# Gated block with expert routing on one Trainium2 core: h of eight units turned by DMA instead of TensorE, x1's rows loaded in pairs, two weight roundings moved to ScalarE

## The chip, the cores and the metric

The kernel runs on one core of a Trainium2 chip. The metric is the device time of one execution in microseconds (us); before the change it is 317.69 us, the median of three runs (317.64 to 318.01).

## What is computed

The reference, cut to what matters:

```python
x = x + tanh(g_xattn) * experts(layernorm(x), token_ids, ctx, ctx, ctx)   # 2048 rows of 512
x = x + tanh(g_ffn)   * ffn(layernorm(x))

def experts(h, ids, Wg, Wu, Wd):        # 4 experts, each weight 512 x 512; here Wg = Wu = Wd = ctx
    e = minimum(clip(ids, 0, 24999) // 6250, 3)
    y_e = (silu(h @ Wg[e].T) * (h @ Wu[e].T)) @ Wd[e].T      # each row takes the y of its own expert

def bit_linear(x, w, b):                # ffn = out(silu(gate(x)) * val(x)), hidden width 2048
    sx = 127 / clip(max|x| of the row, 1e-5);  gw = clip(mean|w|, 1e-5)
    return (clip(round(x * sx), -128, 127) / sx) @ (clip(round(w / gw), -1, 1) * gw).T + b
```

## The kernel before, in words

Every engine has its own program, written out by hand; an engine runs its instructions in that order and waits on semaphores.

**The unit stage (about 24 to 134 us).** The rows are sorted by expert into 19 units of 128 rows, numbered 0 to 18 in the code and in this text (so what the title of the change calls units 10 to 17 are units 9 to 16 here). The loop's step j, called slot j, does on TensorE (`slot`, L609): `turn_gu(j-1)`, four transposes of 128x128 f32; `product` a(j) (L574), twelve matmuls (a high part and a low part in f16 of the turned h against high and low parts of the weight, three passes of four); `turn_h(j+1)` (L558), four transposes of 128x128 f32 of the next unit's h; and `product` y(j-1), twelve matmuls. Around them, for the same slot:

- VectorE (loop after L1144): `gu_low(j-1)` (L1010), `x1_aggr(j-2)`, `gu(j)` (L1005), `h_low(j+1)` (L1001), `norm(j+2)` (L985, writes `h_sb`), `unit_stats(j+3)` (L991), `x1(j-1)` (L1014), `x1_bn_stats(j-1)`.
- ScalarE (`slot`, L804): `gu_hi(j-1)` (L777), `silu(j)` (L773), `h_hi(j+1)` (L769), and between them the work on the feed-forward weights as two tables lay it out: `sum_abs` (L781, sums of |w|, table SUMMED) and `sign_pair` (L792, the ternary weight, table SIGNED).
- GpSimd (loop at L458): the gather of unit j+4, the scatter of x1 of unit j-2 (two for units 8 to 10), `unit_rstd(j+3)`, a small copy, and `round_pair` (L430, table ROUNDED), which scales a pair of weight tiles and rounds it before `sign_pair`.
- SyncE issues, in this order: the twelve loads of 1 MB of the feed-forward weights (L257, the last four each when a gather has landed); the rows of x1, eight tiles of 257.5 KB (L267); the biases (L292 to L294); then the DMA transposes of the next stage (L273, 128x512 bf16; L283, 128x1024 bf16) and the last rows.

**The feed-forward stage (from 134 us)** works on tiles of 128 rows; the change does not touch its code. Its first gate product needs the first 16 sign pairs and the first turned tile of x.

Slots 1 to 14 are written out; slots 15 to 17 are a hardware loop on TensorE.

## Time and profile before

| | |
|---|---|
| median of three runs | 317.69 us |
| the profiled execution's own time | 316.65 us |
| its span, first to last instruction | 314.9 us (1.75 us lie outside it) |
| TensorE busy | 293.4 us, 93% |
| VectorE, ScalarE, GpSimd busy | 262.5, 214.4, 236.7 us |
| mean granted TensorE clock | 0.997 of full |

Times in the rows are microseconds from the span's start. PE is the matmul side of TensorE and PEld its weight loads, DVE is VectorE, ACT ScalarE, POOL GpSimd, SP SyncE; a q behind the name is the engine's sequencer, which issues DMAs. L585 is line 585 of the kernel before. DMA queue q1 is fed by SyncE, q0 by GpSimd's indirect transfers. A page's share of busy time is an average over stages, so the change is read from its own stretch, 67 to 134 us.

### The profile page before, as it was taken

The page shows a single profiled execution, that of the slowest core. Times are in us where ns is not written, and L with a number is a line of the kernel's source. Part 1 is how long each engine was busy: PE and PEld are TensorE (multiplying, and loading weights), DVE is VectorE, ACT ScalarE, POOL GpSimd, SP SyncE. Part 2 cuts the span into 40 slices and gives each one's busy share as a digit, 9 for nine tenths or more (in the row PEclk, how much of TensorE's full clock was granted, in tenths as well). Part 3 has the DMA queues.
Part 4 walks back from the last instruction along what each step waited for, and adds up shares of the span by engine and source line. Part 5 has one row for each costly group of instructions (what it writes and reads, how often), then busy time and mean ns, then how long its engine had stood idle before and what let it go on. Part 6 is the DMA issues. An engine that isn't in the chain of part 4 may idle for free.

```text
span 314.9 us, 5289 instructions
## 1 busy us (share of the span) xinstructions
PE 293.4 (93%) x1424; PEld 142.5 (45%) x1439; DVE 262.5 (83%) x499; ACT 214.4 (68%) x268; POOL 236.7 (75%) x260
## 2 busy tenths in 40 slices
PE   0979999999999999999889899999999999999981
PEld 0435555555555555544334344444444444444430
DVE  5869888868789986789998999998899889988850
ACT  4857688678866456786987788766976687664510
POOL 4554873798888779945776999898888987797722
PEclk9999999999999999999999999999999999999998
DMA  7689899674425822824152754546443542344171
GB/s 265 212 321 335 297 373 325 236 227 180 136 67 170 254 84 84 299 57 89 49 100 50 119 86 123 127 118 146 87 101 83 117 83 71 90 108 100 33 167 67
DMA packets 52549, 47.51 MB, mean 151 GB/s; under 512 B 44783, under 2 KB 44783, under 8 KB 50224
## 3 DMA queue, kind: packets, MB, share of 16 engines
q1 hardware_dynamic: 47968, 33.86, 39.6%
q0 software_dynamic: 4560, 13.40, 12.5%
q8 instruction: 10, 0.16, 0.2%
q14 instruction: 11, 0.09, 0.1%
HBM read 28.35 MB, written 10.00 MB: 122 GB/s over the span
## 4 chain that ended last, share of the span: by engine, by line
PE 82%; DVE 6%; DMA 5%; issue 2%; POOL 2%; ACT 1%; POOLq 0%; DVEq 0%
PE banks L585 31%; PE banks L652 16%; PE banks L661 16%; PE banks L676 14%; PE banks L592 3%; PE banks L562 2%; DMA raw<-in_ctx 2%; DVE raw L1117 1%; POOL w_both L443 1%; DMA out<-xg,raw 1%; DVE raw L1112 1%; DMA xg<-in_x,gather_at 1%; DVE xg L1142 1%; PE banks L548 1%; DMA tok<-in_itok_BxS 1%
## 5 line engine op out<-in xcount | busy, mean ns | idle before, releaser
L585 PE MATMUL banks<-w_both,turned 128*128 x444 | 102.0, 379 | 0.5 <-ACT turned L779 0.3
L443 POOL TENSOR_TENSOR w_both<-raw 128x1024 f32<-128x1024 f32 (+1 forms) x32 | 75.0, 2342 | 9.2 <-DVE raw L1112 7.2
L585 PEld LDWEIGHTS banks<-w_both,turned 128*128 128x128 f16 x444 | 43.4, 98 | 45.5 <-issue 1.6
L854 ACT ACTIVATE w_both<-w_both,magic,raw 128x1024 f32 (+1 forms) x31 | 38.2, 1234 | 36.4 <-DVE raw L1131 36.4
L676 PE MATMUL banks<-tern,xg 128*128 128x512 bf16 x248 | 59.6, 379 | 3.0 <-DVE xg L1142 1.0
L661 PE MATMUL banks<-tern,raw 128*128 128x512 bf16 x255 | 60.3, 379 | 1.3 <-DVE raw L1104 1.3
L652 PE MATMUL banks<-tern,raw 128*128 128x512 bf16 x251 | 59.9, 379 | 0.7 <-DVE raw L1112 0.4
L1104 DVE SCALAR_TENSOR_TENSOR raw<-banks,raw 128x1024 f32<-128x1024 f32 x32 | 40.9, 1278 | 5.7 <-issue 4.9
L1112 DVE SCALAR_TENSOR_TENSOR raw<-banks,raw 128x1024 f32<-128x1024 f32 x32 | 40.9, 1279 | 4.3 <-PE banks L661 4.3
L1117 DVE TENSOR_REDUCE raw<-w_both 128x1 f32<-128x1024 f32 x32 | 38.8, 1212 | 2.7 <-POOL w_both L443 2.6
L676 PEld LDWEIGHTS banks<-tern,xg 128*128 (+1 forms) x256 | 24.8, 98 | 33.7 <-DMA xg<-raw 1.8
L661 PEld LDWEIGHTS banks<-tern,raw 128*128 (+1 forms) x256 | 24.9, 98 | 32.0 <-DVE raw L1104 2.3
L652 PEld LDWEIGHTS banks<-tern,raw 128*128 (+1 forms) x256 | 25.0, 98 | 30.7 <-DVE raw L1112 0.9
L874 ACT ACTIVATE raw<-raw 128x1024 f32<-128x1024 f32 x32 | 33.4, 1045 | 7.0 <-DVE raw L1104 7.0
L490 POOL TENSOR_SCALAR w_both<-w_both,magic,one 128x1024 bf16<-128x1024 f32 x15 | 17.9, 1194 | 15.2 <-ACT w_both L854 15.2
L438 POOL TENSOR_SCALAR raw<-raw,inv_gam,magic 128x1024 f32<-128x1024 f32 x24 | 28.6, 1195 | 0.0
L794 ACT ACTIVATE tern<-raw,magic 128x1024 bf16<-128x1024 f32 x24 | 26.6, 1141 | 0.0
L1007 DVE SCALAR_TENSOR_TENSOR gu_sb<-banks,gu_sb 128x512 f32<-128x512 f32 x19 | 13.1, 687 | 13.8 <-ACT gu_sb L775 13.5
L346 POOL DMA_INDIRECT xg<-in_x,gather_at x19 | 20.3, 1066 | 5.1 <-issue 3.0
L775 ACT ACTIVATE gu_sb<-banks 128x512 f32<-128x512 f32 x19 | 11.3, 596 | 17.8 <-PE banks L585 17.8
L503 POOL DMA_INDIRECT out<-xg,raw x16 | 16.9, 1054 | 8.5 <-DVE xg L1142 6.2
L788 ACT ACTIVATE tern<-raw 128x1024 bf16<-128x1024 f32 x21 | 22.1, 1052 | 0.3
(121 smaller groups left out, 397.5 us busy)
## 6 DMA issues: line engine op xcount, KB each, us to landing
raw<-in_ctx SPq DMA_DIRECT2D x4, 1024.0 KB, 6.5
raw<-in_L_ffn_gate_w SPq DMA_DIRECT2D x4, 1024.0 KB, 7.4
raw<-in_L_ffn_val_w SPq DMA_DIRECT2D x4, 1024.0 KB
raw<-in_L_ffn_out_w SPq DMA_DIRECT2D x4, 1024.0 KB, 5.2
raw<-x_low SPq DMA_DIRECT2D x8, 257.5 KB, 4.4
raw<-x_high SPq DMA_DIRECT2D x8, 257.5 KB, 4.1
raw<-in_L_ffn_gate_b SPq DMA_DIRECT2D x1, 1024.0 KB, 5.4
raw<-in_L_ffn_val_b SPq DMA_DIRECT2D x1, 1024.0 KB, 8.1
```

The costliest lines, as they stand in the source:

```text
L438: nc.gpsimd.tensor_scalar(w, w, inv_gam[:, m:m + 1], magic[:, 0:1], ALU.mult, ALU.add).then_inc(rounded, 1)
L443: nc.gpsimd.tensor_tensor(z[:, t % 2, 2 * D * c:2 * D * c + width], g_sb[:, c, 0:width], v_sb[:, c, 0:width], ALU.mult).then_inc(z_made, 1)
L585: last = nc.tensor.matmul(acc[:, :], a[:, k * P:(k + 1) * P], flat(w[:, bass.ds(e4 + k, 1), :]), start=(k == 0 and i == 0), stop=(k == KD ...
L652: last = nc.tensor.matmul(ring[pair][:, b, :], flat(xiT[:, bass.ds(t % 2, 1), k, :]), tern[:, k * HC + 2 * c + b, :], start=(k == 0), stop ...
L661: last = nc.tensor.matmul(ring[pair][:, b, :], flat(xiT[:, bass.ds(t % 2, 1), k, :]), tern[:, G + k * HC + 2 * c + b, :], start=(k == 0), ...
L676: last = nc.tensor.matmul(to, flat(ziT[:, bass.ds(t % 2, 1), k, :]), tern[:, 2 * G + k, :], start=(k == order[0] * G // 2), stop=(k == (or ...
L794: nc.scalar.activation(flat(tern[:, bass.ds(2 * p, 2), :]), flat(raw[:, bass.ds(2 * p, 2), :]), ACT.Sign, bias=magic[:, 1:2]).then_inc(sig ...
L854: nc.scalar.activation(zq[:, a:b], flat(z[:, bass.ds(t % 2, 1), a:b]), ACT.Identity, scale=flat(sc[:, bass.ds(t, 1), 12:13]), bias=magic[: ...
L874: nc.scalar.activation(g_sb[:, c, :], g_sb[:, c, :], ACT.Silu).then_inc(s_made, 1)
L1104: v.scalar_tensor_tensor(g_sb[:, c, :], flat(ring[(4 * t + 2 * c + 1) % 3 if t else 0]), col(t, 3), bias_g[:, 2 * c * D:2 * (c + 1) * D], ...
L1112: v.scalar_tensor_tensor(v_sb[:, c, :], flat(ring[(4 * t + 2 * c + 2) % 3 if t else 1]), col(t, 4), bias_v[:, 2 * c * D:2 * (c + 1) * D], ...
L1117: v.tensor_reduce(col(t, 5 + c), z[:, t % 2, 2 * D * c:2 * D * (c + 1)], AX.X, ALU.max, apply_absolute_value=True).then_inc(zmax_made, 1)
```

## The change

- For units 9 to 16 (`H_DMA`), VectorE's `norm` writes h into the PSUM bank `hT_ps`; ScalarE's `h_hi` and VectorE's `h_low` make the f16 parts of the rows not yet turned, into `h16` (the bytes of `h_sb`), and SyncE turns both with one DMA transpose of 128x1024 f16 into one of two buffers. TensorE's four transposes for these units are gone, and `product` a(j) waits for the DMA. `norm(j+2)` and `unit_stats(j+3)` come ahead of `gu(j)` in slots 8 to 14, and h is prepared two units ahead.
- SyncE: the turns of units 9 to 14 stand behind the last weight load; then come the waits for the x1 rows, rows 0 and 1, the turn of unit 15, rows 2 and 3, the turn of unit 16, rows 4 to 7.
- ScalarE rounds pairs 8 and 9 itself, in slots 12 and 13, and sums all 24 pairs; VectorE's three `sum_abs` are gone. The tables SUMMED and SIGNED are laid out anew.
- TensorE's slots 15 to 17 are written out. `round_pair` on GpSimd waits load by load.

```diff
-    SUMMED = (0, 0, 2, 5, 8, 11, 13, 14, 15, 16, 18, 20, 21, 21, 21, 21, 21, 21, 21)
+    SUMMED = (0, 0, 2, 5, 8, 10, 13, 15, 16, 17, 18, 20, 22, 24, 24, 24, 24, 24, 24)
     ROUNDED = (0, 0, 0, 0, 0, 0, 2, 4, 6, 8, 8, 9, 10, 12, 14, 16, 20, 24, 24, 24, 24)
-    SIGNED = (0, 0, 0, 0, 0, 0, 0, 2, 4, 6, 8, 8, 9, 10, 12, 14, 16, 17, 18)
+    SIGNED = (0, 0, 0, 0, 0, 0, 0, 1, 3, 5, 7, 8, 9, 10, 12, 14, 16, 17, 18)
+    H_DMA = range(9, 17)
+    ACT_ROUNDS = range(8, 10)
...
+        h16 = h_sb[:, :].bitcast(f16)
+        hT_dma = tern[:, 2 * G + 6:2 * G + 10, :].bitcast(f16).rearrange("p (b i) d -> p b i d", b=2)
...
# SyncE, ahead of the twelve weight loads; called behind them
+            def turn_h(j):
+                sp.wait_ge(hTlo_made, j + 1)
+                if j >= H_DMA[0] + 2:
+                    sp.wait_ge(a_done, j - 1)
+                sp.dma_start_transpose(hT_dma[:, j % 2, :, :].rearrange("p i (k m) -> p (i k) m", m=P), h16).then_inc(h_turned, 16)
...
+            for j in H_DMA[:-2]:
+                turn_h(j)
             sp.wait_ge(signed, x_frees)
             stored_units(EARLY)
             sp.wait_ge(low_scattered, 16 * len(BOTH))
-            for t in range(EARLY):
+            load_rows(0)
+            load_rows(1)
+            turn_h(H_DMA[-2])
+            load_rows(2)
+            load_rows(3)
+            turn_h(H_DMA[-1])
+            for t in range(4, EARLY):
                 load_rows(t)
...
# TensorE, slot
+                    low_made = (hTlo_made, j + 1)
+                    if isinstance(j, int) and j in H_DMA:
+                        low_made = (h_turned, 16 * (j - H_DMA[0] + 1))
+                        pe.wait_ge(*low_made)
+                    else:
+                        pe.wait_ge(hThi_made, j + 1)
...
-                if after:
+                if after and not (isinstance(j, int) and j + 1 in H_DMA):
                     turn_h(j + 1)
...
-            with pe.Fori(GAMMA_SLOT[2] + 1, UNITS - 1) as j:
-                slot(j)
...
# ScalarE
             def h_hi(j):
+                if j in H_DMA:
+                    act.wait_ge(h_made, j + 1)
+                    if j == H_DMA[0]:
+                        act.wait_ge(hT_done, j)
+                    else:
+                        act.wait_ge(h_turned, 16 * (j - H_DMA[0]))
+                    nc.scalar.activation(h16[:, 0:D], hT_ps[:, :], ACT.Copy, scale=H_SCALE).then_inc(hThi_made, 1)
+                    return
...
+            def round_pair(p):
+                m = p // (G // 2)
+                act.wait_ge(gam_made, m + 1)
+                act.wait_ge(raw_loaded[p // 2], 16)
+                w = flat(raw[:, 2 * p:2 * p + 2, :])
+                nc.scalar.activation(w, w, ACT.Identity, scale=inv_gam[:, m:m + 1], bias=magic[:, 0:1]).then_inc(rounded_act, 1)
...
                 silu(j)
-                if 0 < j < UNITS - 1:
+                if 0 < j < UNITS - 1 and j + 1 not in H_DMA:
                     h_hi(j + 1)
+                if j + 2 in H_DMA:
+                    h_hi(j + 2)
...
# VectorE
+                if j in H_DMA:
+                    dve.wait_ge(hTlo_made, j)
+                elif j == H_DMA[-1] + 1:
+                    dve.wait_ge(h_turned, 16 * len(H_DMA))
+                v.tensor_scalar(hT_ps[:, :] if j in H_DMA else h_sb[:, :], unit_rows(j), mean_var[:, n, 0:1], rstd[:, n:n + 1],
...
+                early_norm = j + 1 in H_DMA and j + 2 in H_DMA
+                if early_norm:
+                    norm(j + 2)
+                    unit_stats(j + 3)
                 gu(j)
...
+                if early_norm:
+                    h_low(j + 2)
...
+                if j + 2 in H_DMA and not early_norm:
+                    h_low(j + 2)
...
-                if DVE_SUM <= j < DVE_SUM + PAIRS - ACT_SUMS:
-                    sum_abs(ACT_SUMS + j - DVE_SUM)
```

## Rows read from the trace of the kernel before

**Rows 1.** The page: engines' busy time, and the chain that ended last

```profile
PE 293.4 (93%) x1424; PEld 142.5 (45%) x1439; DVE 262.5 (83%) x499; ACT 214.4 (68%) x268; POOL 236.7 (75%) x260
PE 82%; DVE 6%; DMA 5%; issue 2%; POOL 2%; ACT 1%; POOLq 0%; DVEq 0%
```

**Rows 2.** The chain in order of time (start, us, what), slots 8, 10 and 15

```profile
67.05 0.44 PE banks L592 x4
67.49 2.59 PE banks L585 x12
70.08 0.44 PE banks L562 x4
...
73.10 0.44 PE banks L592 x4
...
79.16 0.44 PE banks L592 x4
...
82.30 0.49 PE banks L562 x4
...
112.80 0.44 PE banks L562 x4
```

**Rows 3.** SyncE's weight loads (ns min/median/max, first and last start us)

```profile
L257 SPq DMA_DIRECT2D raw<-in_L_ffn_out_w x4: 327/328/328, 49.7 to 69.0; - x4
```

**Rows 4.** DMA queues (packets, MB, share of 16 engines), 69 to 73 and 73 to 75 us

```profile
q1 hardware_dynamic: 119, 0.97, 73.9%
...
q0 software_dynamic: 158, 0.52, 66.6%
q1 hardware_dynamic: 25, 0.08, 10.1%
```

**Rows 5.** The 128x1024 DMA transposes: issue ns, landing; DMA busy tenths and q1, 299 to 301 us

```profile
L283 SPq DMA_TRANSPOSE xg<-w_both x30: 1231/1232/1247, 156.9 to 298.3; - x30
DMA to landing us min/median/max: 3.1/3.1/3.8
...
DMA  0000000002599999999999999999999999632000
...
q1 hardware_dynamic: 1056, 0.26, 68.2%
```

**Rows 6.** A transpose behind loads: issue, then packets of 128.5 to 130.5 and 130.5 to 132.5 us

```profile
128.58 6.77 SPq L273 DMA_TRANSPOSE raw<-raw  x2
...
DMA packets 162, 0.81 MB, mean 406 GB/s; under 512 B 26, under 2 KB 26, under 8 KB 88
...
DMA packets 749, 0.62 MB, mean 308 GB/s; under 512 B 580, under 2 KB 580, under 8 KB 748
```

**Rows 7.** Timeline of slot 9 (start, us, engine): ScalarE and VectorE

```profile
76.66 0.59 ACT L771 ACTIVATE turned<-banks 128x512 f16<-128x512 f32 x1
77.14 2.19 ACT L794 ACTIVATE tern<-raw,magic 128x1024 bf16<-128x1024 f32 x2
78.00 0.54 DVE L988 TENSOR_SCALAR h_sb<-xg,mean_var,rstd 128x512 f32<-128x512 f32 x1
79.27 0.74 DVE L1020 SCALAR_TENSOR_TENSOR x_sb<-banks,y_scale,xg 128x512 f32<-128x512 f32 x1
79.63 0.60 ACT L779 ACTIVATE turned<-banks 128x512 f16<-128x512 f32 x1 [0.31 <-issue]
80.12 1.05 ACT L788 ACTIVATE tern<-raw 128x1024 bf16<-128x1024 f32 x1
```

**Rows 8.** Groups by line (busy us, mean ns): the rounding on GpSimd, the nearest on ScalarE

```profile
L438 POOL TENSOR_SCALAR raw<-raw,inv_gam,magic 128x1024 f32<-128x1024 f32 x24 | 28.6, 1195 | 0.0
L854 ACT ACTIVATE w_both<-w_both,magic,raw 128x1024 f32 (+1 forms) x31 | 38.2, 1234 | 36.4 <-DVE raw L1131 36.4
```

**Rows 9.** Matmuls at the start: TensorE ns min/median/max

```profile
L554 PE MATMUL banks<-w_both x23: 379/634/634, 10.0 to 18.1; 128*128 128x512 f16 x23
```

**Rows 10.** Waits (us in total, times, longest): GpSimd for VectorE's unit statistics

```profile
POOL var_eps L382 <- DVE mean_var L999: 14.6, 11, 2.6
```

More of the change, by code:

```diff
@@ L175, in hT_of @@
         def hT_of(j):
+            if isinstance(j, int) and j in H_DMA:
+                return tuple(hT_dma[:, j % 2, i, :] for i in range(2))
             return hTs[isinstance(j, int) and j == 1]
@@ L432, in round_pair @@
                 m = p // (G // 2)
-                if p % (G // 2) == 0:
-                    pool.wait_ge(gam_made, m + 1)
-                    for q in range(4):
-                        pool.wait_ge(raw_loaded[4 * m + q], 16)
+                pool.wait_ge(gam_made, m + 1)
+                if p % 2 == 0:
+                    pool.wait_ge(raw_loaded[p // 2], 16)
                 w = flat(raw[:, 2 * p:2 * p + 2, :])
@@ L460, in _ @@
                 early_rounds = 1 if j < UNITS else 0
+                rounds = [p for p in rounds if p not in ACT_ROUNDS]
                 for p in rounds[:early_rounds]:
@@ L595, in sum_gamma @@
             def sum_gamma(m):
[L597 to L599 removed]
+                pe.wait_ge(abs_summed, G // 2 * (m + 1))
                 pe.wait_ge(consts32, 10)
@@ L638, in _ @@
             slot(0, before=False, after=False, between=turn_second)
-            for j in range(1, GAMMA_SLOT[2] + 1):
+            for j in range(1, UNITS - 1):
                 slot(j, gamma=GAMMA_SLOT.index(j) if j in GAMMA_SLOT else None)
-            with pe.Fori(GAMMA_SLOT[2] + 1, UNITS - 1) as j:
-                slot(j)
             slot(UNITS - 1, after=False)
@@ L1002, in h_low @@
                 dve.wait_ge(hThi_made, j + 1)
-                v.scalar_tensor_tensor(hT_of(j)[1], hT_ps[:, :], H_SCALE, hT_of(j)[0], ALU.mult, ALU.subtract).then_inc(hTlo_made, 1)
+                hi, lo = (h16[:, 0:D], h16[:, D:2 * D]) if j in H_DMA else hT_of(j)
+                v.scalar_tensor_tensor(lo, hT_ps[:, :], H_SCALE, hi, ALU.mult, ALU.subtract).then_inc(hTlo_made, 1)
             def gu(j):
@@ L1154, in _ @@
                     x_gamma(j - EARLY_SLOT - 2)
-                if 0 < j < UNITS - 1:
+                if 0 < j < UNITS - 1 and j + 1 not in H_DMA:
                     h_low(j + 1)
+                if early_norm:
+                    h_low(j + 2)
                 if j > EARLY_SLOT + 1:
@@ L1163, in _ @@
                     gamma(GAMMA_SLOT.index(j))
-                if j + 2 < UNITS:
+                if j + 2 < UNITS and not early_norm:
                     norm(j + 2)
@@ L1167, in _ @@
                     w_low(4)
-                if 2 <= j < UNITS - 3:
+                if 2 <= j < UNITS - 3 and not early_norm:
                     unit_stats(j + 3)
+                if j + 2 in H_DMA and not early_norm:
+                    h_low(j + 2)
                 if j == 5:
                     high_places()
-                if DVE_SUM <= j < DVE_SUM + PAIRS - ACT_SUMS:
-                    sum_abs(ACT_SUMS + j - DVE_SUM)
                 if j == UNITS - 1:
```

30 lines of the change are left out of this document (13 added, 17 removed).

## The prediction

> **What bounds the kernel now.** I read the page first: TensorE is busy 93% of the span and makes 82% of the chain that ended last [rows 1]. Then the same chain in order of time: from slot 2 to slot 18 it never leaves TensorE. A slot is 0.44 (`turn_gu`) + 2.59 + 0.44 (`turn_h`) + 2.59 = 6.06 us: slot 8 begins at 67.05, slot 9 at 73.10, slot 10 at 79.16 [rows 2]. So what TensorE drops there comes off the time, unless a new wait fills it. The other engines wait: ScalarE between its pieces, GpSimd for VectorE's unit statistics 11 times [rows 7, 10]. What must be read next is what a turn by DMA takes on SyncE's queue, and what stands ahead of it there.
>
> **The change part by part.**
>
> TensorE's transposes. Eight groups go, in slots 8 to 15, six at 0.44 us and two at 0.49, the first at 70.08, the last at 112.80 [rows 2], eight such rows: 8 x 0.45 = **-3.6 us**. A slot becomes 5.62 us.
>
> The DMA turn in a quiet slot. The nearest row is the same size in bf16: SyncE spends 1.23 us on the issue, it lands 3.1 to 3.8 us after it, and its data are moving for 1.36 us of all 16 engines (68.2% of 2 us), ending about 0.5 us ahead of the landing: the digits stop near 300.9, the landing of the issue at 298.3 is 301.4 [rows 5]. `h_low(j+2)` ends some 5.1 us into slot j: a(j) ends at 3.03, then silu 0.6, `h_hi` 0.5, `h_low` 0.7 and gaps. So the turn is issued at 5.2 and lands at 8.3 to 9.0, while a(j+2) begins at 2 x 5.62 + 0.44 = 11.7. The cover is 2.7 us or more. ScalarE's `h_hi(j+3)` asks for it earlier, 5.62 + 3.7 = 9.3 us: just enough. Cost 0.
>
> The first turn, unit 9. This one isn't quiet. In SyncE's program it stands behind the twelfth weight load, which starts at 69.0 [rows 3], for it waits for the gather of unit 11, which the change doesn't touch. So the turn is issued at about 69.4, right behind 1 MB. That load keeps q1's engines busy until after 73: 119 packets in 69 to 73, the last 25 in 73 to 75, while gather and scatter on q0 take 66.6% of 73 to 75, or 1.33 us of all engines [rows 4]. Does a transpose wait for loads ahead of it on its queue? One row can tell: turn_x(0), issued at 128.58 behind the bias loads, has hardly any small packets in the first 2 us (26) and 580 in the next 2, when the loads are done [rows 6]; a quiet one moves its packets 1.1 to 2.6 us after the issue [rows 5]. So it waits. From 73.0 on there remain 0.2 (load) + 1.33 (q0) + 1.36 (turn) = 2.9 us, to 75.9, and 0.5 to the landing: 76.4 if the turn is last of all. If q0 took nothing from it: 73.4 + 1.36 + 0.5 = 75.3. I take **76.0**, nearer to the end where both share, since q0 is served all through 73 to 75.
> TensorE wants it at 73.10 - 0.44 + 0.44 = 73.1: it stands for **2.9 us** (2.2 to 3.3).
>
> What queues up behind that wait. ScalarE's `h_hi(10)` waits for the same turn, because both use `h16`; behind it stand two sign pairs (2.19 us) and `gu_hi(8)` (0.6) [rows 7]. Counted from the landing L: `h_hi` starts at L+0.05, the signs at L+0.53, `gu_hi(8)` at L+2.65, ready at L+3.2; TensorE is through a(9) at L+2.65, so it stands **0.6 us** more for y(8). Then VectorE: `gu_low(8)` at L+3.25, `norm(11)`, `unit_stats(12)` and `gu(9)`, each of 0.5 to 0.9 us, end at L+6.05, where y(8) ended at L+5.85: **0.2 us** more. Slot 10 so begins at L+6.05 = 82.05, against 79.16 before [rows 2]: 2.9 us late. From there the lag is gone: ScalarE has 5.1 us of work (1.8 + one sum 1.1 + two signs 2.2) in slots 9 and 10 each.
> With the 6 groups of slots 10 to 15 (2.7 us) the stage ends 2.9 - 2.7 = **0.2 us later** than before. In other terms: 3.8 us of stands (with roundings) against 3.6 saved.
>
> ScalarE in slots 12 and 13. Its own three pieces 1.8 us, two sums (1.05 and the read of the sum, 1.14 with it) 2.3, a sign pair 1.1, and the new rounding, whose nearest rows are 1.23 (ScalarE, same tile) and 1.20 (GpSimd) [rows 7, 8]: 6.4 us in a slot of 5.62, twice. Lag 1.6 us; `gu_hi` may come 1.9 us late (turned at 0.44, needed at 3.03, 0.6 long). With waits between the pieces `gu_hi(13)` ends about where it is needed: **+0.2 us**, between 0 and 1.6. Slot 14 has 4.0 us and takes it back. VectorE loses three sums and gets `norm` writing PSUM, an operation the trace lacks; PSUM-touching ones of this size take up to 0.74 against 0.54 [rows 7], so at most 0.2 a unit, with some 0.3 free ahead of `gu`. GpSimd loses 2 x 1.2 us [rows 8]; it waits for VectorE anyway [rows 10], cost 0. If its two-round passes should bind, the cover is the whole slot by which `rstd` runs ahead.
>
> Rows of x1 and turns 15 and 16. Two tiles of 257.5 KB ahead of a turn are half the load that delays unit 9, and are issued some 3 us before the turn is ready; the turn has 2.7 us of cover more. Cost 0, up to 0.5. Rows 4 to 7 land near 117, about when GpSimd wants them. Writing out slots 15 to 17: 0. The feed-forward stage hangs on TensorE's last unit slot and moves with it.
>
> Sum, against the profiled 316.65: -3.6 + 3.8 + 0.2 = +0.4, so 317.0; the median of the runs lies 1.04 above the profiled execution: 318.05, told as **318.0**.
>
> A rule that speaks against this change: the Trainium skill, page "VectorE: DVE Perf Modes", section on rules for kernel authors, says to use TensorE for a 128x128 transpose where PSUM will do as its target, and its section on the three transpose paths gives 1309 ns for one by DMA. Eight such blocks one after another would be 10.5 us a unit, and the slots would be bound by it: an estimate from that page, 8 x (10.5 - 6.06) = +36 us. The trace disagrees: eight blocks land in 3.1 us [rows 5].
>
> **The rivals.**
>
> A. The turn lands in time everywhere, unit 9 too. For: nothing in the code orders the data of two transfers. Against: [rows 6], and q1's engines are full up to 73 anyway [rows 4]. Then -3.6 + 0.2: **314.3**. Chance 0.10.
>
> B. The wait is there, but at its short end and without followers: L = 75.3, the signs don't hold `gu_hi(8)`. -3.6 + 2.2 + 0.1 = -1.3: **316.4**. For: bounds above. Against: the order of ScalarE's program. Chance 0.08.
>
> C. Slower: ScalarE, late from unit 9's turn, doesn't recover before slots 12 and 13, and their overload falls on TensorE in full. It decides once ScalarE enters slot 12 more than 0.3 us late, for then all 1.6 us show, through `gu_hi`, and some 0.4 more by `silu` and `gu`. 318.0 - 0.2 + 2.0: **319.8**. For: 5.1 and 5.2 of 5.62 us in slots 10 and 11 leave little to recover with. Against: slot 9's slack. Chance 0.12.
>
> D. Slower: TensorE's clock falls in the stand at unit 9. The first matmuls of the run, after idle time, took 634 ns at median against 379 later [rows 9], the lower of the two levels (1.2 and 2.4 GHz); no idle stretch of 3 us occurs later. Some 12 to 16 matmuls at 0.21 us more: +3.0, **321.0**. Chance 0.04. The Trainium skill, page "TensorE: Matmul & The Clock Gate", Part 1, has the clock fall after idle time; by that rule D is what a stand at the long end would give, and no row here shows it.
>
> **How the numbers follow.** The forecast's case has 0.66; its own range is 317.3 to 318.8 (L from 75.3 to 76.4, ScalarE's 0 to 0.6). The range that should hold 8 in 10 leaves out A, D and the far edges: 316.2 to 319.6. A measurement of this kernel can tell some 0.2%, 0.64 us, from no change: same is 317.05 to 318.33. Faster: A, B and 0.04 of the forecast's case, 0.22. Slower: C, D and 0.22 of it, 0.38. Same: the other 0.40.
>
> **What would show it.** In the profile after: no L562 rows in slots 8 to 15 and slots of 5.62 us (right), TensorE idle some 3 us before a(9), released by the DMA or by ScalarE's chain, ScalarE idle as long before `h_hi(10)`; the small packets of the first turn after 73.4; slot 10 beginning near 82. The prediction is wrong if the first turn's packets move by 71 to 72.5 (A), if stands appear at slots 13 and 14 (C), or if matmuls after the stand take over 600 ns (D).

## The result and the profile after

The changed kernel takes **322.48 us** (median of 4 runs, 321.74 to 325.57) against 317.85 of the kernel before on the same chip (317.64 to 318.94): ratio 1.0147, 95% interval 1.0095 to 1.0198. It is slower by 4.6 us, where no change was forecast. Its profiled execution took 322.68 us with a span of 320.9, against 316.65 and 314.9 of before: 6.0 us to explain.

The page of the changed kernel, busy time and the chain that ended last [rows 1]:

```profile
PE 295.2 (92%) x1406; PEld 139.5 (43%) x1406; DVE 261.9 (82%) x496; ACT 219.4 (68%) x276; POOL 234.2 (73%) x258
...
PEclk9999999997999999999999999999999999999978
...
PE 71%; DMA 10%; DVE 9%; issue 3%; ACT 2%; POOL 2%; POOLq 0%; DVEq 0%; SPq 0%; ACTq 0%
```

TensorE has fewer instructions and is busy 1.8 us longer (the trace of before lacks 14 of its matmul records, so the difference isn't exact). The PEclk line says why: two dips, one in the slice near 76 us and one in the last two; the very last slice dips in before too, behind its last matmul. DMA has gone from 5% of the chain to 10%.

The chain in order of time, slots 9 and 10 [rows 2]:

```profile
69.82 0.33 SPq L269
...
70.19 6.39 DMA tern<-h_sb
...
76.71 7.04 PE banks L606 x24
83.75 0.44 PE banks L613 x4
```

The turn of unit 9, issued right behind the twelfth weight load, lands 6.39 us later, and the chain runs through it. The timeline of the same stretch (start, us, engine, line; in brackets the idle time and what ended it) [rows 7]:

```profile
73.34 0.66 PE L613 MATMUL banks<-ident,gu_sb 128*128 128x128 f32 x4
...
76.67 0.60 ACT L798 ACTIVATE h_sb<-banks 128x512 f16<-128x512 f32 x1 [4.75 <-DMA tern<-h_sb]
76.71 4.45 PE L606 MATMUL banks<-w_both,tern 128*128 x12 [2.72 <-DMA tern<-h_sb]
...
80.55 0.78 DVE L1037 TENSOR_SCALAR banks<-xg,mean_var,rstd 128x512 f32<-128x512 f32 x1
81.00 2.75 PE L606 MATMUL banks<-w_both,turned 128*128 x12
```

TensorE stands 2.72 us, and then the twelve matmuls of a(9) take 4.45 us, where twelve take 2.75 in the next row. Windows of 3 us (busy time of PE, PEld, DVE, ACT, POOL, then the granted clock, DMA share, GB/s) show it:

```profile
73.00:76.00 3.00, 0.94 (x6) 0.42 (x4) 0.28 (x1) 0.00 (x0) 2.89 (x5) 1.00 1.09 318
76.00:79.00 3.00, 2.29 (x6) 0.91 (x7) 1.67 (x3) 2.33 (x3) 1.48 (x3) 0.65 0.39 133
79.00:82.00 3.00, 3.00 (x12) 1.23 (x11) 2.48 (x6) 2.66 (x6) 1.49 (x2) 0.78 0.77 175
```

The eight turns, by their line (duration of the issue; landing min/median/max) [rows 5]:

```profile
L258 SPq DMA_TRANSPOSE tern<-h_sb x8: 1232/1236/1331, 70.2 to 113.5; - x8
...
DMA to landing us min/median/max: 3.1/3.4/6.4
```

The slowest is the first. The next slowest are those issued at 83.3 and 100.1, with 4.7 and 5.3 us to the landing; more of them below.

The other half is at the end of the program, which the change doesn't touch. The last two DMA transposes and the last 16 matmuls, first of before, then of the changed kernel:

```profile
300.88 2.61 SPq L283 DMA_TRANSPOSE xg<-raw  x2
301.38 1.90 PE L676 MATMUL banks<-tern,xg 128*128 128x512 bf16 x8 [0.64 <-DMA xg<-w_both]
304.17 3.75 PE L676 MATMUL banks<-tern,xg 128*128 128x512 bf16 x16 [0.90 <-DMA xg<-raw]
```

```profile
304.07 3.37 SPq L295 DMA_TRANSPOSE xg<-raw  x2
304.57 1.90 PE L698 MATMUL banks<-tern,xg 128*128 128x512 bf16 x8 [0.64 <-DMA xg<-w_both]
308.60 5.31 PE L698 MATMUL banks<-tern,xg 128*128 128x512 bf16 x16 [2.13 <-DMA xg<-raw]
```

From the issue of the pair to the last 16 matmuls it takes 3.29 us before and 4.53 after, and the 16 take 5.31 instead of 3.75. What else is on the queues there, 305 to 306.5 us of the changed kernel:

```profile
q1 hardware_dynamic: 944, 0.24, 84.6%
q8 instruction: 1, 0.02, 3.9%
```

One packet of q8 lies among those of the transposes. The page has 11 such packets with 0.18 MB in the whole run, 16 KB each, and calls their kind "instruction". They come 13 to 31 us apart, but for 84 us (191 to 275) in which TensorE goes round its loop of the feed-forward stage. I read them as the fetch of TensorE's next instructions; experiments 5 and 10, which add instructions to TensorE and nothing else, move them. In before the last was at 282 us. In the changed kernel it is at 306. Two more lie beside the two slow turns named above, at 85.3 and 103.4.

**Where 6.0 us went.** I took the start of each slot from the timelines (`turn_gu`'s first matmul) and subtracted. Slot lengths in us, and the part from the last `turn_gu` to the end of the span:

| slot | 8 | 9 | 10 | 11 | 12 | 13 | 14 | 15 | 16 to 18 | end part |
|---|---|---|---|---|---|---|---|---|---|---|
| before | 6.05 | 6.05 | 6.23 | 6.05 | 6.06 | 6.05 | 6.23 | 6.05 | 17.86 | 181.4 |
| after | 6.15 | 10.25 | 5.75 | 5.62 | 5.61 | 5.62 | 6.73 | 5.93 | 17.86 | 184.2 |

Slots 8 to 18 are 2.9 us longer (+4.20 in slot 9; -1.8 in slots 10 to 13; +0.5 in slots 8, 14 and 15 together), the end part 2.8, and 0.3 lies ahead of slot 8.

### The profile page after: what moved, and what is told of

It is laid out like the page before. It is cut to its first block, busy times and chain, and to the rows that moved or that the text cites. A ratio compares the mean times of both kernels' runs of the same rounds, so it can differ in the third digit from the quotient of the medians.

```text
span 320.9 us, 5259 instructions
## 1 busy us (share of the span) xinstructions
PE 295.2 (92%) x1406; PEld 139.5 (43%) x1406; DVE 261.9 (82%) x496; ACT 219.4 (68%) x276; POOL 234.2 (73%) x258
## 4 chain that ended last, share of the span: by engine, by line
PE 71%; DMA 10%; DVE 9%; issue 3%; ACT 2%; POOL 2%; POOLq 0%; DVEq 0%; SPq 0%; ACTq 0%
PE banks L606 22%; PE banks L674 16%; PE banks L683 16%; PE banks L698 14%; DMA tern<-h_sb 4%; DMA xg<-in_x,gather_at 3%; DMA raw<-in_ctx 2%; PE banks L613 2%; DMA out<-xg,raw 1%; DVE raw L1162 1%; POOL w_both L463 1%; DVE raw L1157 1%; PE banks L583 1%; DVE xg L1187 1%; PE banks L569 1%
## 5 line engine op out<-in xcount | busy, mean ns | idle before, releaser
L606 PE MATMUL banks<-w_both,turned 128*128 x348 | 80.0, 379 | 1.1 <-ACT turned L809 0.8
L698 PE MATMUL banks<-tern,xg 128*128 128x512 bf16 x256 | 61.5, 387 | 3.8 <-DMA xg<-raw 2.1
L606 PEld LDWEIGHTS banks<-w_both,turned 128*128 128x128 f16 x348 | 34.0, 98 | 38.3 <-issue 3.3
L606 PE MATMUL banks<-w_both,tern 128*128 x108 | 26.6, 398 | 3.3 <-DMA tern<-h_sb 2.7
L458 POOL TENSOR_SCALAR raw<-raw,inv_gam,magic 128x1024 f32<-128x1024 f32 x22 | 26.2, 1192 | 0.0
L820 ACT ACTIVATE tern<-raw 128x1024 bf16<-128x1024 f32 x24 | 25.3, 1053 | 0.3
```

What stands on the lines that cost most here:

```text
L458: nc.gpsimd.tensor_scalar(w, w, inv_gam[:, m:m + 1], magic[:, 0:1], ALU.mult, ALU.add).then_inc(rounded, 1)
L606: last = nc.tensor.matmul(acc[:, :], a[:, k * P:(k + 1) * P], flat(w[:, bass.ds(e4 + k, 1), :]), start=(k == 0 and i == 0), stop=(k == KD ...
L698: last = nc.tensor.matmul(to, flat(ziT[:, bass.ds(t % 2, 1), k, :]), tern[:, 2 * G + k, :], start=(k == order[0] * G // 2), stop=(k == (or ...
```

## The experiments

Sixteen kernels were run, in four groups, each group on one chip with runs of the kernel before beside it (its medians 318.01, 318.32, 317.54 and 317.70). Single runs of one kernel scatter by some 2 us either way (before: 315.97 to 320.34), so a reading rests on the profile's slot lengths, with the ratio beside it. Part of that scatter lies ahead of the change: in the profiled executions of experiments 5, 6, 8, 9, 10 and 12 slot 3 is 6.65 to 7.80 us long instead of 6.05, and in that of 4 slot 4 is 7.40. In 9 TensorE stands 1.46 us there for VectorE's x1, and VectorE stood 2.73 us for a gather that landed late. The change isn't needed for it (kernels 4 and 10 are the kernel before at that place), nor are the short matmuls of some kernels (4 and 6 have none). But five of the six long slots 3 stand in kernels with short matmuls at the start, so a tie to these isn't ruled out. "End part" is always the time from the last `turn_gu` to the end of the span.

### 1. The turn of unit 9 ahead of the weight load

```diff
             for n in range(12):
+                if n == 11:
+                    turn_h(H_DMA[0])
...
-            for j in H_DMA[:-2]:
+            for j in H_DMA[1:-2]:
                 turn_h(j)
```

> Only edit to the changed kernel: unit 9's turn is issued ahead of the twelfth weight load instead of behind it. Theory Q (the turn's data wait behind 1 MB on the same queue): it lands 3.1 to 3.8 us after its issue at about 68.7, so by 72.5; TensorE's stand of 2.7 us ahead of a(9) and ScalarE's of 4.75 are gone, and with the stand the 12 matmuls at half clock (4.45 us for 2.6). Slot 18 then begins near 126 instead of 131.1 (127.9 before). For the end there are two theories. F: the late transpose landing at the end (4.5 us against 3.3 before) comes from a TensorE instruction fetch that falls on it, and it stays, as TensorE's program is the same length: about 317.5. N: the end was chance: 315.0. Rival to Q (a first DMA transpose is slow by itself): the stand stays and the time is about 322.

Measured: 317.61 us, ratio 0.9973 (0.9939 to 1.0007). Slot 9 takes 5.94 us instead of 10.25:

```profile
71.30 2.76 PE L608 MATMUL banks<-w_both,turned 128*128 x12 [0.15 <-ACT turned L811]
74.11 0.66 PE L615 MATMUL banks<-ident,gu_sb 128*128 128x128 f32 x4
74.68 1.30 SPq L258 DMA_TRANSPOSE tern<-h_sb  x1
74.86 2.76 PE L608 MATMUL banks<-w_both,tern 128*128 x12
```

No stand, and the clock stays up. So the place on SyncE's queue costs the stand, and this one edit takes back the whole loss of the unit stage: its slots 8 to 18 sum to 65.3 us, 4.2 less than in the changed kernel and 1.3 less than before's 66.6. The first row shows a small thing: slot 8 has no `turn_h(9)`, yet it keeps 6.16 us, because y(7) now waits for ScalarE. The end part is still 182.5, with a q8 packet at 303 us and 2.09 us of stand; here the last 16 matmuls took 3.63 us, so the clock stayed up.

### 2. Turns by DMA from unit 10 on

```diff
-    H_DMA = range(9, 17)
+    H_DMA = range(10, 17)
```

> Only edit: the turned units are 10 to 16, seven instead of eight; unit 9 is turned on TensorE as before. Theory Q: the turn of unit 10 is issued when the weight load is done, no stand, seven times 0.45 us saved: slot 18 begins 0.5 us later than with unit 9's turn moved ahead, about 126.5. By F the end still costs some 2.8 us (318.0), by N not (315.5). Rival to Q (a first transpose is slow by itself): a stand of some 2.7 us now stands ahead of a(10), about 322.

Measured: 319.84 us, ratio 1.0048 (1.0016 to 1.008), profiled 318.05. No stand at unit 10: its turn is issued at 74.4, and a(10) begins at 79.88. Slot 9 takes 6.16 us. Slots 10 to 12 stayed at 6.16, 6.27 and 6.01, so this kernel has less of the saving than the count of its turns says (its last `turn_gu` is at 133.7, and the expectation for the unit stage missed by 1.5 us). TensorE waits there in short gaps, the longest 0.26 us for ScalarE's `gu_hi`; the rest isn't explained. The end part is 182.6: its q8 packet is at 303 us, and TensorE stands 2.20 us. The first slot without `turn_h` doesn't get shorter, neither here (slot 9) nor in experiment 1 (slot 8).

### 3. TensorE kept busy in the stand

```diff
                         low_made = (h_turned, 16 * (j - H_DMA[0] + 1))
+                        if j == H_DMA[0]:
+                            keep_warm(12)
                         pe.wait_ge(*low_made)
```

> Only edit: 12 matmuls of 128x512 on a free bank, ahead of the wait for unit 9's turn, so that TensorE works while it would stand. Theory C (TensorE's clock fell because of the stand): a(9)'s matmuls take 379 ns again, 2.6 us instead of 4.45, and slot 10 begins near 82.0 instead of 83.75; the end as in the changed kernel or moved by the 24 instructions more; 320.7. Rival (the slow matmuls of a(9) have another cause, as their operands just landed by DMA): they stay at over 600 ns and the time is 322.5.

Measured, in the profiled execution (319.36 us): slot 9 takes 8.83 us instead of 10.25.

```profile
74.39 2.76 PE L575 MATMUL banks<-w_both 128*128 128x512 f16 x12
76.99 2.75 PE L606 MATMUL banks<-w_both,tern 128*128 x12
```

```profile
76.00:79.00 3.00, 3.00 (x16) 1.35 (x15) 1.86 (x3) 2.52 (x3) 2.06 (x3) 1.00 0.29 111
```

Same landing of the turn (6.42 us), granted clock 1.00, a(9) in 2.75 us instead of 4.45. The clock's share of slot 9 is 1.4 (the slots) to 1.7 us (the matmuls). Its median, 322.98 of 4 runs (319.36 to 327.32; ratio 1.018, 1.0099 to 1.0262), says nothing of a gain: the stand itself varies between executions. The profiled ones with the turn behind the load have 2.72 us (changed kernel), 2.38 (experiment 5), 1.63 (11) and 6.75 (14).

### 4 and 5. The unrolling alone, and instructions added

The kernel before with slots 15 to 17 written out as the change has them:

```diff
-            for j in range(1, GAMMA_SLOT[2] + 1):
+            for j in range(1, UNITS - 1):
                 slot(j, gamma=GAMMA_SLOT.index(j) if j in GAMMA_SLOT else None)
-            with pe.Fori(GAMMA_SLOT[2] + 1, UNITS - 1) as j:
-                slot(j)
```

> The kernel before with one part of the change alone: TensorE's slots 15 to 17 written out. Theory F: some 170 instructions more ahead of the end, so its last fetch, at 282 before, comes at about 264 and one more at about 292, ahead of the last transposes by 8 us: no change of the time, 0 to 0.3 us. Rival (written-out slots cost more than a loop): each of slots 15 to 17 longer than 6.06 us, 318.5 or more.

Measured: 317.51 us, ratio 0.9964 (0.9938 to 0.999). Slots as before, but for slot 4; the last q8 packets moved to 268 and 293 us, clear of the last transposes; end part 181.3. The unrolling alone costs nothing, and by itself it does not bring a fetch to 306 us either. That takes the other part of the change with it: the turns of eight units, 64 instructions fewer ahead of the end.

The changed kernel with 48 short matmuls (96 instructions with their weight loads) at TensorE's start:

```diff
             pe.wait_ge(consts16, 3)
+            for _ in range(48):
+                nc.tensor.matmul(a_ps[:, 0:4], ones16[:, :], ones16[:, 0:4], start=True, stop=True)
```

> Only edit: 48 tiny matmuls in TensorE's idle time at the start, 96 instructions more in its program. Nothing moves in the unit stage. Theory F (an instruction fetch of TensorE that falls on the last DMA transposes makes them land late): the last fetch, at 305.5 in the changed kernel, moves some 10 us ahead, to 293 to 297; the last transposes land 3.3 us after the issue, the clock stays up: 319.7 to 320. Theory N (chance, or something else of the change): the end stays slow, 322.5.

Measured: 321.77 us, ratio 1.0095 (1.0067 to 1.0123), profiled 322.96. The last q8 packet is at 295; the last 16 matmuls begin 3.29 us after the issue of the pair and take 3.84 us, as in before. But the time is not won: packets now lie on the turns issued at 78.5 and 95.0, which land 4.5 and 5.2 us after their issue instead of 3.1 and 3.7, and slot 13 takes 6.93; one more at 136 us falls on the first x transposes of the feed-forward stage, and TensorE stands 1.46 us there (end part 183.1). The expectation of 319.7 to 320 missed. Adding instructions at the start moves every fetch at once. The stand at unit 9 was 2.38 us in this execution, and the granted clock did not fall behind it: a(9) took 2.76 us and slot 9 took 9.09.

### 6 and 7. The two roundings

The kernel of experiment 1 with both roundings back on GpSimd:

```diff
-    ACT_ROUNDS = range(8, 10)
...
-                rounds = [p for p in rounds if p not in ACT_ROUNDS]
...
+                act.wait_ge(rounded, p + 1)
```

> Edit on the kernel with unit 9's turn ahead of the last weight load: GpSimd again rounds pairs 8 and 9. Theory S (two sums, a rounding and a sign are too much for ScalarE in slots 12 and 13, and it shows in slot 14, 6.57 us long where 5.82 would do): slot 14 comes back to 5.9, the unit stage ends 0.7 us earlier; about 317.0. Rival FU (slot 14 is long because an instruction fetch at 99.3 falls on unit 14's turn, and h_hi(15) waits for it): slot 14 stays above 6.3 us, 317.6.

Measured: 317.62 us, ratio 0.998 (0.995 to 1.0011). Slot 14 falls from 6.57 to 5.75 us, so ScalarE's work has a part in it. Slots 16 and 17 rise to 6.31 and 6.77 for a reason that I hadn't thought of:

```profile
121.69 0.78 ACT L903 ACTIVATE banks<-raw 128x512 f32<-128x512 f32 x1 [2.40 <-POOL raw L438]
122.41 2.17 ACT L833 ACTIVATE tern<-raw,magic 128x1024 bf16<-128x1024 f32 x2
124.49 0.57 ACT L809 ACTIVATE turned<-banks 128x512 f16<-128x512 f32 x1
```

GpSimd's step for the first tile (L438) has slid behind the roundings, ScalarE waits 2.40 us for it, and `gu_hi` and two signs are queued behind that wait. This is a cost of the roundings on GpSimd with shorter slots. The sum is a draw. Its turn of unit 14 has a fetch beside it as in experiment 1, so the rival that this fetch alone makes slot 14 long is out.

The roundings alone on ScalarE, in the kernel before:

```diff
+    ACT_ROUNDS = range(8, 10)
...
+                rounds = [p for p in rounds if p not in ACT_ROUNDS]
```

> The kernel before with one part of the change alone: ScalarE rounds pairs 8 and 9, in slots 12 and 13, the rest as before. Theory S: in the slots of 6.06 us with at most one sum beside it ScalarE has 5.3 us of work, so nothing shows: within 0.3 us of the kernel before, slots 12 to 14 at 6.06, 6.05 and 6.23. Rival (the rounding on ScalarE costs by itself, 1.24 us each): slots 13 and 14 longer by 0.5 or more, 318.7.

Measured: 318.75 us, ratio 1.001 (0.998 to 1.0041); slots 6.05 to 6.23 as before. In slots of 6.06 us ScalarE has room for them; in slots of 5.62 it hasn't.

### 8, 9 and 12. Early turn with more instructions at the start

Experiment 1 with 15 (8) and 57 (9) short matmuls at the start, and (12) with 57 and eight more matmuls ahead of the wait for the last transposes.

> Edit on the kernel with unit 9's turn ahead of the last weight load: 15 tiny matmuls in TensorE's idle time at the start, 30 instructions more, so that its fetches come some 3.3 us sooner. Theory F: the last fetch falls at about 299, ahead of the last two transposes (issued at 300.6 and 302), which land 3.3 us after the issue again; the end, from TensorE's last unit transposes to the last instruction, is 181.4 to 181.7 us instead of 182.5, and those of the unit stage fall between turns: 316.3. Rival N: the end stays at 182.5, 317.6.

> The kernel after with the turn of unit 9 issued ahead of the twelfth weight load, and 57 short matmuls (114 instructions) at TensorE's start, so that its program is fetched at other moments: by the spacing of the earlier traces at about 73, 91 and 288 us instead of 81, 99 and 302. Theory F (a fetch of TensorE's instructions during a DMA transpose lengthens it): no turn of h and not the last pair of transposes has a fetch beside it; the last pair lands within 3.4 us of its issue, the part behind the last turn of gu takes 181.3 us instead of 182.5, the turns land after 3.1 to 3.7 us; median about 1 us below the kernel before, 316 to 317. Rival (the end is late for another reason, such as the order in which the feed-forward stage finds its weights): the part behind the last turn of gu stays at 182.4 to 183.4 us, and the median stays at 317.5.

> The kernel with the early turn of unit 9 and the 57 short matmuls at the start, and eight matmuls of 512 columns ahead of TensorE's wait for the last two transposes (1.7 us). If the transposes are in time (0.9 us of stand) the eight matmuls cost 0.8 us and the time lies that much above the kernel without them; if they are late, they cost nothing and keep the clock up. Both theories: unit stage as in the kernel without them, 1.5 to 2 us shorter than before; median 316 to 317.5.

Measured: 317.48 us (ratio 0.9972, 0.9933 to 1.0012), 318.21 (1.0018, 0.9993 to 1.0043) and 318.43 (1.0035, 1.0007 to 1.0064). All three expectations on the total missed. In each a fetch fell at another place; slot 3 was long in the profiled executions of all three as well (7.10 to 7.80 us), and that costs as much again. The edit at TensorE's start (57 in place of 15 in 9 and 12), and that of 12 at its end:

```diff
+            for _ in range(15):
+                nc.tensor.matmul(a_ps[:, 0:4], ones16[:, :], ones16[:, 0:4], start=True, stop=True)
...
+            for _ in range(8):
+                nc.tensor.matmul(o_of(t), tern[:, 2 * G, 0:P], tern[:, 2 * G + 1, :], start=True, stop=True)
             down(t, 1, to=o_of(t), order=(1, 0))
```

In 8 the q8 packet came at 300.7 us and fell on the transposes of 298.7, one pair earlier: 2.13 us of stand, the clock fell, end part 183.4. In 9 and 12 the last transposes were in time as expected (0.91 us of stand in 9), but a packet at 131 us fell on the first x transposes. Of experiment 9:

```profile
128.41 9.23 SPq L287 DMA_TRANSPOSE raw<-raw  x2
133.35 0.60 PE L617 MATMUL banks<-ident,gu_sb 128*128 128x128 f32 x4
135.51 1.90 PE L678 MATMUL banks<-tern,raw 128*128 128x512 bf16 x8 [1.55 <-DMA raw<-raw]
```

That is 1.55 us of stand where before has none, and the end part is 183.1. The slots, 5.62 to 5.97 from 9 to 15, were as good as foreseen.

These two also tell the causes of the long slot 14 apart. In 9 and 12 ScalarE has both roundings, and no fetch lies behind the issue of unit 14's turn, which lands after 3.7 us: slot 14 takes 5.97. In experiment 6 it has neither, with the turn late: 5.75. In experiment 1 it has both, with the turn late: 6.57. So either alone costs 0.2 us or less, and the two together 0.8.

### 10 and 15. A fetch put onto the last transposes of the kernel before

The kernel before, nothing of the change in it, with 43 (10) and 60 (15) short matmuls at the start:

```diff
+            for _ in range(43):
+                nc.tensor.matmul(a_ps[:, 0:4], ones16[:, :], ones16[:, 0:4], start=True, stop=True)
```

> The kernel before, nothing of the change in it, with 43 short matmuls (86 instructions) at TensorE's start. The last fetch of its program was at 282 us and the one behind it would have been past the end, 31 us later; 86 instructions more bring that one to about 302.5, onto the last two transposes (issued 300.9). Theory F: these land 4.4 to 4.6 us after their issue instead of 3.3, TensorE stands about 2.1 us instead of 0.9 ahead of the last 16 matmuls, the part behind the last turn of gu takes 182.5 us (clock stays up) to 184.2 us (it falls) instead of 181.4; the slots of the unit stage stay 6.05 to 6.23. Rival: 3.3 us and 181.3 us as before, so that the long end comes from the change's own work.

> The kernel before with 60 short matmuls (120 instructions) at TensorE's start, 34 instructions more than in the kernel whose last fetch was at 275 us: the one behind it comes at about 302 us, onto the last two transposes (issued about 301 to 302.7). Theory F: they land 4.4 to 4.6 us after issue, TensorE stands about 2.1 us instead of 0.9, and the part behind the last turn of gu takes 182.5 us (the clock stays up) to 184.2 us (it falls) instead of 181.4, with nothing of the change in the kernel. Rival: 181.4 us. If the fetch misses them again: 181.4 us by both, and no answer.

Measured: in 10 the last packet is at 275 us and none follows; end part 181.3, ratio 1.0016 (0.9989 to 1.0043). It missed its aim and tells only that the short matmuls cost nothing that the times show; slot 3 took 7.31 us in its profiled execution. In 15 packets came at 271 and 301 us:

```profile
301.77 2.61 SPq L283 DMA_TRANSPOSE xg<-raw  x2
303.76 7.01 PE L678 MATMUL banks<-tern,xg 128*128 128x512 bf16 x24 [2.13 <-DMA xg<-w_both]
```

and in 300.5 to 302.5 us:

```profile
q1 hardware_dynamic: 962, 0.24, 63.0%
q8 instruction: 1, 0.02, 2.8%
```

TensorE stands 2.13 us, the end part is 183.3 instead of 181.4, the slots are 6.05 to 6.23 as in before, and the median is 319.02 beside 317.70 (ratio 1.0023, 0.9993 to 1.0052, so the times alone show no difference; the profile does). It hit the pair ahead of the last one and not the last, but it shows the point: a long end comes without any of the change's work, by where the fetch falls.

How much of it is the clock, the profile of experiment 3 tells. There a fetch fell on the same pair, and TensorE stood 2.09 us:

```profile
305.29 5.35 PE L700 MATMUL banks<-tern,xg 128*128 128x512 bf16 x24 [2.09 <-DMA xg<-w_both]
```

The clock stayed up, the 24 matmuls took 5.35 us instead of 7.01, and the end part is 181.7. So at this pair the late landing itself costs 0.3 us and the clock 1.7.

### 11. TensorE kept busy ahead of the last transposes

```diff
             t = TILES - 1
+            for _ in range(10):
+                nc.tensor.matmul(o_of(t), tern[:, 2 * G, 0:P], tern[:, 2 * G + 1, :], start=True, stop=True)
             down(t, 1, to=o_of(t), order=(1, 0))
```

> The kernel after with ten matmuls of 512 columns on a free bank ahead of TensorE's wait for the last two transposes (2.2 us at the upper clock). If the granted clock falls because TensorE stands there: the last 16 matmuls take 3.7 us instead of 5.3 and the profiled execution ends 1.2 to 1.6 us earlier, 321.2, with the transposes still landing 4.4 us after their issue and the stand at unit 9 as before (slot 9 at 10.2 us). If it falls for another reason, the last 16 stay at 5 us. Against this: if the transposes are in time the ten matmuls themselves cost up to 1 us.

Measured: 320.8 us, ratio 1.0098 (1.0062 to 1.0134), profiled 320.88.

```profile
303.99 3.42 SPq L295 DMA_TRANSPOSE xg<-raw  x2
304.49 1.90 PE L698 MATMUL banks<-tern,xg 128*128 128x512 bf16 x8 [0.64 <-DMA xg<-w_both]
306.23 2.32 PE L747 MATMUL banks<-tern 128*128 128x512 bf16 x10
308.53 3.63 PE L698 MATMUL banks<-tern,xg 128*128 128x512 bf16 x16
```

The transposes are still late (308.53 is 4.54 us after the issue), but the last 16 take 3.63 us instead of 5.31 and the end part is 182.5 instead of 184.2. So the 2.8 us of the end are 1.2 for the late landing and 1.6 for the clock. Slot 9 took 8.34 us in this execution and not the expected 10.2: the stand was 1.63 us, and no fall of the clock followed.

### 13 and 14. The fetch moved inside the feed-forward stage

54 short matmuls at three places where TensorE stood 0.41, 0.42 and 0.88 us for VectorE, so that the unit stage keeps its program. 13 has the early turn as well, 14 only this:

```diff
+            def short(count):
+                for _ in range(count):
+                    nc.tensor.matmul(o_ps[:, 0:4], ones16[:, :], ones16[:, 0:4], start=True, stop=True)
...
-            ffn_slot(2, 0, downs=False)
-            ffn_slot(3, 1, start_down=True)
+            ffn_slot(2, 0, downs=False, shorts=(13, 13))
+            ffn_slot(3, 1, start_down=True, shorts=(28, 0))
```

> The kernel after with the turn of unit 9 issued ahead of the twelfth weight load, and 54 short matmuls (13, 13 and 28) in the feed-forward stage, at three places where TensorE stood 0.41, 0.42 and 0.88 us for VectorE, on a bank that nothing uses there. The unit stage keeps its program and so its fetches; the later fetches come some 10 us sooner (about 262 and 290 us, not 271 and 302). Theory F (a fetch during a DMA transpose lengthens it): the last two transposes land 3.3 us after their issue, TensorE stands 0.9 us there instead of 2.1, the part behind the last turn of gu takes 181.2 to 181.6 us instead of 182.5, slots 13 and 14 stay at 5.8 and 6.6; profiled time near 316.3, median 0.5 to 1.2 us below the kernel before. Rival (the end is late for another reason): 182.5 us.

> The kernel after, with only the same 54 short matmuls in the feed-forward stage. Theory F: the fetch of 305 us comes at about 293; the last two transposes land 3.3 us after issue, the last 16 matmuls take 3.7 us, the part behind the last turn of gu takes 181.2 to 181.6 us instead of 184.2; the stand at unit 9 stays (slot 9 at 8.3 to 10.3 us), so the profiled time is 318.6 to 320.2. Rival: 183 to 184 us behind the last turn of gu, and 322.

Measured, 13: **316.19 us**, ratio 0.9951 (0.9925 to 0.9977), profiled 315.46. The last packets are at 261 and 286 us, and

```profile
299.80 2.61 SPq L297 DMA_TRANSPOSE xg<-raw  x2
300.30 1.90 PE L700 MATMUL banks<-tern,xg 128*128 128x512 bf16 x8 [0.64 <-DMA xg<-w_both]
303.07 3.66 PE L700 MATMUL banks<-tern,xg 128*128 128x512 bf16 x16 [0.88 <-DMA xg<-raw]
```

with an end part of 181.4. Slot 14 is still 6.63 us.

14: 319.44 us, ratio 1.0044 (1.0014 to 1.0075), against 1.0147 of the changed kernel; end part 181.2. The end is mended with nothing else touched, and what is left is the unit stage. Its runs lie between 317.57 and 324.61. The profiled one, 324.19, is one of the two longest, and shows what made it so:

```profile
80.44 5.27 PE L606 MATMUL banks<-w_both,tern 128*128 x12 [6.75 <-DMA tern<-h_sb]
```

In this execution the turn of unit 9 landed 9.7 us after its issue, not 6.4, and TensorE stood 6.75 us; slot 9 took 15.1, and the expectation (8.3 to 10.3) missed. The load isn't the whole reason: its last packet ends at 75.8 us, against 75.1 in the changed kernel. But of the turn's packets 179 come after 76.5, up to 79.9, beside those of GpSimd's transfers, where in the changed kernel none comes after 76.0:

```profile
q0 software_dynamic: 120, 0.40, 70.5%
q1 hardware_dynamic: 179, 0.04, 7.2%
```

(76.5 to 80 us.) Why they came so late isn't shown, nor how often it happens: the other runs have no trace.

### 16. One of the two roundings back on GpSimd

Experiment 13 with

```diff
-    ACT_ROUNDS = range(8, 10)
+    ACT_ROUNDS = range(8, 9)
```

> The kernel with the early turn of unit 9 and the 54 short matmuls in the feed-forward stage, and of the two roundings only the first (pair 8) on ScalarE, the second back on GpSimd. With both on ScalarE slots 13 and 14 took 5.8 and 6.6 us; with both on GpSimd slots 16 and 17 took 6.3 and 6.8, because ScalarE stood 2.4 us for a step of GpSimd that had slid behind the roundings. Theory: each rounding on ScalarE costs the slots 13 and 14 about half of 0.9 us, so slot 14 is near 6.1 us and slots 16 and 17 near 6.1 and 6.3: no gain or up to 0.5 us. Rival (the long slot 14 is the late turn of 96.8 us alone, with a fetch beside it): slot 14 stays at 6.5 us or more.

Measured: **314.58 us** (6 runs, 314.25 to 315.37), ratio 0.9892 (0.986 to 0.9923): 3.1 us faster than the kernel before and 1.6 faster than experiment 13. Slots 13 to 15 take 5.76, 6.08 and 5.62 us (5.65, 6.63 and 5.94 in 13), 16 and 17 stay at 6.05. The timeline of ScalarE in slots 13 and 14:

```profile
101.61 0.60 ACT L806 ACTIVATE h_sb<-banks 128x512 f16<-128x512 f32 x1 [1.08 <-DMA tern<-h_sb]
102.11 1.05 ACT L828 ACTIVATE tern<-raw 128x1024 bf16<-128x1024 f32 x1
103.06 0.19 ACT L828 ACTIVATION_READ_ACCUMULATOR tern<-raw 128x1 f32 x1
103.15 1.14 ACT L845 ACTIVATE tern<-raw,magic 128x1024 bf16<-128x1024 f32 x1
104.19 0.58 ACT L817 ACTIVATE turned<-banks 128x512 f16<-128x512 f32 x1
```

The turn is just as late as in 13 (a packet of q8 lies beside it; it lands 5.6 us after its issue, 5.2 in 13), yet without the rounding of 1.23 us between sum and sign `gu_hi` ends 3.16 us after the start of `h_hi` (104.77) and not 4.43 (105.56). So slot 14 was ScalarE's overload behind a late turn, both of them, and the rival that it was the late turn alone falls. The profiled executions differ by 0.77 us (314.69 against 315.46), which the slots account for (0.75); the medians differ by more, and that rest isn't explained.

## Why the prediction was wrong, step by step

The forecast was 318.0, between 316.2 and 319.6. It came to 322.48. Against the forecast's sum (317.0 for the profiled execution, 322.68 measured) 5.7 us are missing:

| step | forecast, us | measured | missed |
|---|---|---|---|
| quiet turns, slots 10 to 13 | -1.8 | -1.8 | 0 |
| slot 8 | -0.45 | +0.1 | 0.55 |
| stand at unit 9 and followers, less the group of slot 9 | +3.3 | +4.2 | 0.9 |
| slots 14 and 15, and ScalarE's overload | -0.7 | +0.4 | 1.1 |
| feed-forward stage "moves with it" | 0 | +2.8 | 2.8 |
| ahead of slot 8 | 0 | +0.3 | 0.3 |

- **Quiet turns: right.** Five of the eight land in 3.1 to 3.7 us, and slots 11 to 13 take the forecast 5.62 us; the one issued at 83.3, which lands after 4.7, has cover enough. On the rule about transposes by DMA that the prediction names, the trace of the changed kernel says the same as [rows 5]: a quiet turn of eight blocks lands in 3.1 us.
- **The queue behind the weight load: right.** [rows 6] told it. Landing 6.39 us after the issue, 6.6 forecast; stand 2.72 us, 2.9 forecast. Rival A falls with the packets: from 72 to 74.4 us q1 moves 94 of 8 KB and none under 512 B, and 1072 of these come by 76. Experiment 1 shows that the order on the queue is the cause. That the stand came so near is in part luck, as it was 1.63 to 6.75 us in the other executions with this order. The followers were over-sized: with the clock up (experiment 3) slot 9 took 8.83 us where the forecast's steps give 9.4.
- **The clock, rival D, came at a chance of 0.04.** This is the first failed step. The stand was forecast at nearly 3 us, [rows 9] showed matmuls at the lower level behind idle time, and "no idle stretch of 3 us occurs later" in the kernel before was a reason to take the risk seriously, not to set it low. It was over-sized too: 1.4 to 1.7 us and not 3.0, because the twelve matmuls of a(9) took 0.14 us more each (4.45 instead of 2.75 us together) and not 0.21, the clock coming back meanwhile (granted 0.65 from 76 to 79 us, 0.78 from 79 to 82). The Trainium skill, "TensorE: Matmul & The Clock Gate", Part 1, has the clock fall after idle time. The trace agrees at 2.72 us of stand. Of the four profiled stands at this place (1.63, 2.38, 2.72 and 6.75 us, in experiments 11 and 5, the changed kernel and experiment 14) the two longer ones brought a fall and the two shorter ones did not. So the chance was nearer to one half than to 0.04.
- **Slot 8: a saving that a queue took.** I subtracted 0.45 us from every slot. In the first one ScalarE's `h_hi(9)` stands 1.79 us for VectorE's `norm(9)`, and `gu_hi(7)` behind it comes later than TensorE now asks for it. The slack of ScalarE's pieces was read for slot 9 only [rows 7].
- **ScalarE's work of slots 12 and 13: the term was mis-sized.** The sum of its pieces, 6.4 us in 5.62, was right, and so was the upper bound of 1.6; I took 0.2, because I let the waits between the pieces absorb it. Its lag stood in slots 14 and 15. Experiments 13 and 16 show 0.75 us for the second of the two roundings alone. But it took a second cause, which the forecast didn't have: the turn issued at 100.1 landed 5.3 us after its issue, with a fetch behind it, while the forecast had called a landing by 3.8 us "just enough" for the next `h_hi`. With that turn in time (experiments 9 and 12) both roundings leave slot 14 at 5.97. Rival C isn't it: slots 11 to 13 are at 5.62, so the lag of unit 9's stand was gone, and slot 14 is as long in experiment 1, which has no such stand.
- **"The feed-forward stage moves with it": the largest failed step, and it had no bounds.** I costed the unrolling and the missing turns by their own work. The unrolling costs none (experiment 4), but both change the length of TensorE's program, and with it where the fetches fall: with the unrolling alone the last is at 293 us, with both it is at 306, onto the last pair of transposes, where TensorE has no cover at all (it stands 0.90 us there even before). Experiment 15 shows a long end with nothing of the change, 14 that moving the fetch mends it, 11 that 1.6 of the 2.8 us are the clock.
- GpSimd and VectorE: cost 0 as forecast, as the roundings alone change no slot (experiment 7) and slots 11 to 13 take 5.62 us. `norm` into PSUM took 0.78 us, against 0.54 [rows 7]: 0.24 more, at most 0.2 forecast.

What stays open: why the clock fell behind 2.13 us of stand in the changed kernel's end and not behind 2.09 in experiment 1's; why slots 10 to 12 of experiment 2 kept their length; and the rest of the gain of experiment 16.

## What to carry to other kernels

Before a transfer is put on a queue, read what stands ahead of it there at that moment, and move the short one ahead of the long one where its data allow it: one line was worth some 3 us here (medians of experiments 13 and 14; their kernels differ in nothing else). Price a stand of some 2 us or more with the clock's fall behind it as a matter of chance, and treat a saving per slot as void in the slots where another engine's queue already ends near the need. When a change alters the length of an engine's program, compare where its instruction fetches fall with the transfers on which that engine waits with little cover, to the end of the program, not only where the code changed.

## What the runs showed of the hardware that was not expected

- **A fetch of TensorE's instructions (16 KB, one packet of q8) makes a DMA transpose beside it late.** Over the profiled executions of all 18 kernels, the landings of 580 transposes of 128x1024 can be read. 507 have no such packet beside them: 500 land 3.0 to 3.9 us after the issue, the other seven are those behind or close behind other loads on the queue (4.3 to 9.7). 35 have one that starts 0.4 to 2.3 us after their issue, in 14 of the kernels: all land late, after 3.5 to 5.2 us. Of those with a packet later than 2.3 us most are not late (3.0 to 3.3), but five turns of the unit stage (5.2 to 5.6) and one more (4.6) are. A packet that starts ahead of the issue or within 0.2 us behind it makes no difference. At the end of the changed kernel 944 packets of q1 lie in 305 to 306.5 us, beside the fetch, and only 17 in 307.0 to 307.5, and the landing comes 1.2 us later than in before. Why so small a transfer does this, the traces don't show.
- **The clock's fall is not told by the length of the stand alone.** 2.72 us gave 0.65 granted behind it; 2.13 us gave 0.50 (309 to 312 us, changed kernel):

```profile
309.00:312.00 3.00, 3.00 (x8) 1.03 (x7) 0.75 (x1) 0.00 (x0) 0.76 (x1) 0.50 0.33 133
```

  and 2.09 us in experiment 1 gave no fall, 16 matmuls in 3.63 us. Nor did 2.09 in experiment 3, 2.20 in 2 and 2.38 in 5, while 2.13 did in 8 and 15, and just ahead of the unit stage 1.94 and 2.00 did in 7 and 11, but 1.97 in 1 did not. One fall cost 1.4 to 1.7 us in the changed kernel (each of its two) and in experiment 15; behind the 6.75 us of experiment 14 a(9) alone took 2.5 us more.
- **A DMA transpose queued behind a 1 MB load** landed 6.4 us after its issue in the profiled execution of the changed kernel, 6.5 in experiment 5's and 9.7 in experiment 14's, where a quiet one takes 3.1. The 9.7 are not the load's alone, as the packets of experiment 14 show.
